# A second routed FFN merged into the program of a recurrence, its gelus cut into halves behind two scan steps

## The chip, the cores and the metric

The kernel runs on one core of a Trainium2 chip. The metric is the device time of one execution in microseconds (us). The profile is of one more execution; its time is given beside its span.

## What is computed

The input x has 4 sequences of 1024 positions and 128 features, in float32. `ln` is a layer norm without weights.

```python
x = x + 0.5 * L0_ffn(ln(x))     # routed FFN: per position a small attention over the 4 sequences,
                                # then top 2 of 8 experts, gelu (tanh form), 128 -> 256 -> 128
x = x + L0_attn(ln(x))          # hierarchical attention
x = x + 0.5 * L0_ffn(ln(x))     # the same routed FFN again
x = x + 0.5 * L1_ffn(ln(x))     # binarised weights, exact gelu, 128 -> 512 -> 128     ("a")
x = x + L1_attn(ln(x))          # recurrence over the 1024 positions                   ("p", "r")
x = x + 0.5 * L1_ffn(ln(x))     # the binarised FFN again                              ("z")

def step(state, inp):           # inside L1_attn, 1024 times, state [4 x 32]
    xb_t, xd_t = inp
    state = tanh(state @ A.T + xb_t)
    return state, state @ C.T + xd_t
# then y = layernorm(out + x) * w + b, and y + gelu(y W1 + b1) W2 + b2
```

Each routed FFN acts on a position by itself. So do the FFNs a and z. Only the recurrence has an order over positions.

## The kernel before

x stays in SBUF as `x_all`, in 8 groups of 128 positions by 4 sequences. The kernel is written for each engine by hand, with semaphores, and runs four programs one after the other (`PHASES`, L1947): routed FFN (`causal_moe_ffn`, L31), attention, routed FFN, and then `binarize` (L546) with `second_half` (L597). A program begins when all engines have ended the one before.

**The routed FFN** works through the 8 groups. For each of 8 experts PE makes two chunks of hidden values (`up_products`, L270, one product of 512 columns a chunk, in a ring of three PSUM banks), ScalarE makes each chunk's gelu in one instruction of 512 columns (L193), PE multiplies back (`down_products`, L279, 8 products of 128 columns into one of two banks), and VectorE adds the expert with its weight into x (`add_expert`, L456). Between the experts stand the steps of later groups: transposes (`p_turn1`, `p_turn2`, `p_turn3`), the query-key-value product (`p_qkv`, L239, two banks in turn), projection and router, and their norms on VectorE with the power -1/2 on GpSimd.

**`second_half`** holds the scan. `body(g)` (L921 on PE, L997 on ScalarE) is made for each group g and has 128 steps. A step is one product on PE, `r_scan<-r_state,rnnA` (L941: 4 columns, 32 outputs), and one tanh on ScalarE (L1006) whose result is the next step's input. After each step's product stands at most one other piece of PE work, at the step that the table `SLOTS` gives it: a product or transpose of 128 columns. The pieces of body g are a(g+2), p(g+1), r(g-1) and z(g-1): `turn_piece`, `up_piece`, `down_piece`, `mix_piece`, `input_piece`. ScalarE makes each gelu of those FFNs as four instructions of 128 columns behind four tanhs (`gelu_piece`). Each engine executes its instructions in the order written, so that a wait of one holds up all behind it, the scan's too.

The last group's r and z come after the last step.

Of the kernel before, what the change touches and what calls it, by code (L numbers as in the profile page):

```python
# [545 lines left out]
def binarize(nc, S):  # L546

    with ExitStack() as ctx:
        sgn = ctx.enter_context(nc.sbuf_tensor("sgn", [128, 2, FC, 128], F32))
        alpha = ctx.enter_context(nc.sbuf_tensor("alpha", [128, FC + 1], F32))  # L550
        banks = [ctx.enter_context(nc.psum_tensor(f"bin_turn{i}", [128, 512], F32)) for i in range(2)]
        s_sign, s_bin, s_turn = (ctx.enter_context(nc.semaphore(n)) for n in ("signs", "binarised", "bin_turned"))
        w1 = S["bin1"][:, :].rearrange("p (c d) -> p c d", d=D)
        w2 = S["bin2"][:, :].rearrange("p (c h) -> p c h", h=128)
        with nc.Block() as block:
            @block.scalar
            def _(act):
                for i, w in enumerate((w1, w2)):
                    nc.scalar.activation(sgn[:, i, :, :], w, ACT.Sign).then_inc(s_sign, 1)

            @block.vector
            def _(dve):

                dve.tensor_reduce(alpha[:, 0:FC], w1, AX.X, ALU.add, apply_absolute_value=True)
                dve.tensor_reduce(alpha[:, FC:FC + 1], w2, AX.XY, ALU.add, apply_absolute_value=True)
                dve.drain()
                dve.tensor_scalar(alpha[:, 0:FC], alpha[:, 0:FC], 1.0 / D, None, ALU.mult)
                dve.tensor_scalar(alpha[:, FC:FC + 1], alpha[:, FC:FC + 1], 1.0 / (FC * 128), None, ALU.mult)
                dve.drain()
                dve.wait_ge(s_sign, 2)  # L570
                for i, w in enumerate((w1, w2)):
                    for c in range(FC):
                        a = alpha[:, c:c + 1] if i == 0 else alpha[:, FC:FC + 1]
                        dve.scalar_tensor_tensor(sgn[:, i, c, :], sgn[:, i, c, :], a, w[:, c, :],
                                                 ALU.mult, ALU.subtract)
                dve.drain()
                for i, w in enumerate((w1, w2)):
                    dve.tensor_tensor(sgn[:, i, :, :], sgn[:, i, :, :], w, ALU.add).then_inc(s_bin, 1)

                rows = S["rows"]  # L580
                dve.tensor_tensor(rows[:, 1, :], rows[:, 1, :], rows[:, 2, :], ALU.add)
                dve.tensor_scalar(rows[:, 3, :], rows[:, 3, :], 0.5, None, ALU.mult)
                for i, n in enumerate(("bin1", "bin2")):
                    dve.wait_ge(s_turn, i + 1)
                    dve.tensor_copy(S[n][:, :], banks[i][:, :])

            @block.tensor
            def _(pe):
                for i in range(2):
                    pe.wait_ge(s_bin, i + 1)  # L590
                    for c in range(FC):
                        last = nc.tensor.transpose(banks[i][:, c * 128:(c + 1) * 128], sgn[:, i, c, :],
                                                   S["ident"][:, :])
                    last.then_inc(s_turn, 1)
# [1384 lines left out]
```

## Time and profile before

| | us |
|---|---|
| median of 3 runs | 2226.37 (2222.71 to 2226.94) |
| the profiled execution | 2226.66 |
| its span, first to last instruction | 2224.9 |
| PE busy | 1851.9 (83%) |
| DVE busy | 1009.9 (45%) |
| ACT busy | 862.7 (39%) |
| POOL busy | 193.9 (9%) |
| mean granted TensorE clock | 0.735 |

All times inside the program are us from the span's start. A granted clock of 1.00 is 2.4 GHz and one of 0.50 is 1.2 GHz, the two levels that occur; a mean between them says that a stretch had both. PE is TensorE's products, PEld its weight loads, DVE is VectorE, ACT ScalarE, POOL GpSimd. A float32 product leaves two MATMUL records and two LDWEIGHTS records, a float32 transpose one of each. "Busy" counts a record from its issue to its end.

### The profile page before, as it was taken

The numbers are of one execution on the slowest core, as the hardware profiler recorded it, in microseconds if no ns is written. First come the engines' busy times: TensorE is split into PE (matmuls) and PEld (weight loads), VectorE is DVE, ScalarE is ACT, GpSimd is POOL, SyncE is SP. The second block draws the span as 40 slices with busy tenths as digits, with TensorE's granted clock in tenths as the row PEclk, the third lists the DMA queues.
The fourth block names the chain that finished last, engine by engine and source line by source line (L and its number), as shares of the span: only waits on it lengthen the run. The fifth ranks groups of instructions, "written<-read, shape, count | busy, mean of one in ns | idle before, by whom it ended". The sixth has DMA issues, their size and how long they took to land. (4 is left out here: it accounts for less than half of the span.)

```text
span 2224.9 us, 37410 instructions
## 1 busy us (share of the span) xinstructions
PE 1851.9 (83%) x13672; PEld 1372.4 (62%) x13672; DVE 1009.9 (45%) x3005; ACT 862.7 (39%) x2377; POOL 193.9 (9%) x314
## 2 busy tenths in 40 slices
PE   1889896848858588558898977799999999999886
PEld 1666675447556485546666765576777777766665
DVE  3666754775866778746666642111111111111102
ACT  1434442745546456424353432232323232323231
POOL 1211201001010010012121100000000000000000
PEclk8999996969879799779999985555555555555556
DMA  6000000000000000000000000000000000000000
GB/s 156 1 1 0 0 1 1 2 1 3 2 1 3 2 2 2 1 1 1 1 0 1 1 1 1 1 1 5 1 6 1 5 1 5 1 5 1 5 1 10
DMA packets 12015, 13.03 MB, mean 6 GB/s; under 512 B 1648, under 2 KB 10640, under 8 KB 11280
## 3 DMA queue, kind: packets, MB, share of 16 engines
q1 hardware_dynamic: 11840, 10.77, 1.8%
q8 instruction: 101, 1.65, 0.3%
q14 instruction: 74, 0.61, 0.1%
HBM read 8.67 MB, written 2.10 MB: 5 GB/s over the span
## 5 line engine op out<-in xcount | busy, mean ns | idle before, releaser
L1006 ACT ACTIVATE r_state<-r_scan 32x4 f32<-32x4 f32 x1024 | 166.9, 163 | 592.6 <-PE r_scan L941 589.3
L941 PEld LDWEIGHTS r_scan<-r_state,rnnA 128*32 128x32 f32 x2048 | 186.3, 141 | 253.3 <-issue 153.6
L941 PE MATMUL r_scan<-r_state,rnnA 128*32 128x4 f32 x2048 | 275.4, 205 | 52.1 <-ACT r_state L1006 52.1
L286 PEld LDWEIGHTS f_down<-moe,f_hT 128*128 128x128 f32 x2048 | 251.3, 194 | 56.9 <-issue 54.0
L277 PE MATMUL f_up<-f_x2T,moe 128*128 128x512 f32 x512 | 248.8, 610 | 11.6 <-ACT f_hT L193 11.6
L286 PE MATMUL f_down<-moe,f_hT 128*128 128x128 f32 x2048 | 254.0, 278 | 0.0
L463 DVE SCALAR_TENSOR_TENSOR x_all<-f_down,f_weight,x_all 128x128 f32 (+1 forms) x512 | 144.1, 344 | 166.6 <-PE f_down L286 163.9
L193 ACT ACTIVATE f_hT<-f_up 128x512 f32<-128x512 f32 x256 | 149.9, 598 | 139.0 <-PE f_up L277 137.6
L1618 DVE TENSOR_TENSOR att_big<-at_ring,att_big 128x512 f16<-128x512 f32 x192 | 123.9, 685 | 49.2 <-ACT att_big L1300 48.4
L277 PEld LDWEIGHTS f_up<-f_x2T,moe 128*128 128x128 f32 x512 | 90.5, 195 | 90.0 <-issue 63.5
L1300 ACT ACTIVATE att_big<-at_ring 128x512 f16<-128x512 f32 x192 | 111.4, 596 | 66.5 <-PE at_ring L1433 64.6
L761 DVE TENSOR_TENSOR x_all<-r_post_misc,x_all 128x512 f32<-128x512 f32 x8 | 5.5, 692 | 233.4 <-PE r_post_misc L845 233.4
L1433 PE MATMUL at_ring<-at_keys,att_Mhi 128*128 128x512 f16 x256 | 81.7, 403 | 30.2 <-DVE at_coarse_q L1605 18.6
L833 PE MATMUL r_up_post<-r_nT_r,mlp 128*128 128x128 f32 x256 | 94.9, 483 | 1.3 <-DVE r_nT_r L725 0.9
L845 PE MATMUL r_post_misc<-bin,r_h_post 128*128 128x128 f32 x256 | 93.1, 474 | 1.2 <-ACT r_h_post L976 1.2
L845 PE MATMUL r_post_misc<-mlp,r_h_post 128*128 128x128 f32 x256 | 93.1, 474 | 1.2 <-ACT r_h_post L976 1.2
L1725 DVE SCALAR_TENSOR_TENSOR att_big<-at_ring,att_big 128x512 f16<-128x512 f32 x128 | 80.8, 682 | 27.2 <-ACT att_big L1341 27.1
L1523 PE MATMUL at_s<-att_Nhi,att_big 128*128 128x128 f16 x1024 | 92.8, 222 | 0.0
L1341 ACT ACTIVATE att_big<-at_ring 128x512 f16<-128x512 f32 x128 | 68.7, 602 | 61.4 <-PE at_ring L1514 61.0
L1523 PE MATMUL at_s<-att_Nlo,att_big 128*128 128x128 f16 x512 | 89.3, 222 | 0.0
L1452 PEld LDWEIGHTS at_s<-at_keys,att_big 128*128 128x128 f16 x768 | 64.5, 99 | 38.4 <-issue 19.5
L1452 PE MATMUL at_s<-at_keys,att_big 128*128 128x16 f16 x768 | 72.1, 172 | 18.5 <-DVE att_big L1618 18.5
(241 smaller groups left out, 3202.2 us busy)
## 6 DMA issues: line engine op xcount, KB each, us to landing
x_all<-in_x SPq DMA_DIRECT2D x4, 512.0 KB, 6.1
moe<-in_moe SPq DMA_DIRECT2D x2, 1024.0 KB, 7.1
out<-x_all SPq DMA_DIRECT2D x8, 256.0 KB, 2.3
bin<-in_bin SPq DMA_DIRECT2D x2, 256.0 KB, 7.6
mlp<-in_mlp SPq DMA_DIRECT2D x2, 256.0 KB, 6.0
att_big<-in_att_wq SPq DMA_DIRECT2D x1, 512.0 KB, 11.2
att_big<-in_att_wk SPq DMA_DIRECT2D x1, 512.0 KB, 13.2
att_big<-in_att_wv SPq DMA_DIRECT2D x1, 512.0 KB, 14.9
```

The source lines that it names most:

```text
L193: nc.scalar.activation(hT[c % H_RING][:, :], up[c % UP_RING][:, :], ACT.Gelu_apprx_tanh).then_inc(s_h, 1)
L277: nc.tensor.matmul(up[c % UP_RING][:, :], w1[:, c * 128:(c + 1) * 128], x2T[b][:, :], start=True, stop=True).then_inc(s_up, 1)
L286: last = nc.tensor.matmul(down[e % 2][:, s * 128:(s + 1) * 128], hT[c % H_RING][:, s * 128:(s + 1) * 128], w2[:, c * 128:(c + 1) * 128], s ...
L463: last = dve.scalar_tensor_tensor(xg[:, s, :], down[e % 2][:, s * 128:(s + 1) * 128], weight[b][:, s, e:e + 1], xg[:, s, :], ALU.mult, ALU ...
L833: ins = nc.tensor.matmul(UP[k][c % len(UP[k])][:, s * 128:(s + 1) * 128], W1[k][:, c * 128:(c + 1) * 128], nT[k][g % 2][:, s * 128:(s + 1) ...
L845: ins = nc.tensor.matmul(MISC[k][:, s * 128:(s + 1) * 128], H[k][c][:, s * 128:(s + 1) * 128], W2[k][:, c * 128:(c + 1) * 128], start=(c = ...
L941: nc.tensor.matmul(scan[b][0:STATE, NB * t:NB * (t + 1)], rnnA[:, :], last, start=False, stop=(t == 127), skip_group_check=True).then_inc( ...
L1006: nc.scalar.activation(state[b][0:STATE, NB * t:NB * (t + 1)], scan[b][0:STATE, NB * t:NB * (t + 1)], ACT.Tanh).then_inc(s_tanh, 1)
L1300: nc.scalar.activation(XH[c % 2][:, :, h, :], ring[n % RING][:, :].rearrange("p (q i) -> p q i", i=BLK), ACT.Copy).then_inc(s_xhi, 1)
L1452: nc.tensor.matmul(o, lh, keys[:, blk, 0, :], start=True, stop=False)
L1523: last = nc.tensor.matmul(sbk[t % 2][:, 0:D], y[t % 2][:, h, :], att[w][:, h * D:(h + 1) * D], start=(h == 0 and n == 0), stop=(h == HEADS ...
L1618: dve.tensor_tensor(XL[c % 2][:, :, h, :], ring[n % RING][:, :].rearrange("p (q i) -> p q i", i=BLK), XH[c % 2][:, :, h, :], ALU.subtract) ...
```

## The change

The third and fourth program become one, `routed_ffn_and_recurrence`. It computes the same. The second routed FFN runs two groups ahead of the scan: groups 0 and 1 before the first step, group m = g + 2 inside body g, for g from 0 to 5. The binarised weights are prepared at the program's start. Body g also holds a(g+1), p(g+1), r(g-1) and z(g-2); before, it was a(g+2), p(g+1), r(g-1), z(g-1). z of group 6, r of 7 and z of 7 come after the last step.

With one program there are 8 PSUM banks for all: two for the scan, two for `up` (a ring of three before), one `down` (two before), one `turn` for every transpose and small product of the routed FFN (three before), and `post_misc` and `pre_misc`. The FFNs a, r and z use `up`, `up` and `down` in turn.

The order on PE is no longer a table of steps. `slots(g)` writes the items of a body in a row with a length in ns for each and spreads them evenly over the 128 steps. An item is larger than a piece: half a chunk (256 columns), an expert's tile (2 products of 128 columns), a dense tile (4 such products), all four transposes of a group. Gelus are two instructions of 256 columns behind two tanhs.

```diff
-PHASES = ("ffn", "attn", "ffn", "second")
+PHASES = ("ffn", "attn", "rest")
...
+            def p_turn1(pe, f):
+                pe.wait_ge(s_xn1, ONE + f + 1)
+                pe.wait_ge(s_stats2, ONE + f)
+                turn_tiles(xn1, s_turn1, turn)
...
+            def p_qkv(pe, f, s):
+                if s == 0:
+                    pe.wait_ge(s_ln1T, ONE + f + 1)
+                pe.wait_ge(s_qkv, ONE + NB * f + s)
+                nc.tensor.matmul(turn[:, 0:QKV], ln1T[:, s * 128:(s + 1) * 128], wqkv[:, :],
+                                 start=True, stop=True).then_inc(s_q, 1)
...
+            def down_tile(pe, m, e, s):
+                if s == 0:
+                    pe.wait_ge(s_h, ONE + CHUNKS * m + 2 * e + 2)
+                    pe.wait_ge(s_add, ONE + EXPERTS * m + e)
...
+            def k_up_half(pe, k, g, c, half, before):
...
+                    elif before is None:
+                        m = clip(g + 2 if k == "a" else GROUPS)
+                        pe.wait_ge(s_h, ONE + CHUNKS * m)
+                        pe.wait_ge(s_add, ONE + EXPERTS * m)
...
+            NS = {up_half: 480, down_tile: 500, k_turn_tiles: 1000, p_turn1: 1000, p_turn2: 1000, p_turn3: 1000,
+                  p_qkv: 740, p_proj: 1000, p_router: 500, k_up_half: 480, k_down_tile: 1000, input_product: 900,
+                  mix_tiles: 1000}
...
+            def slots(g):
+                order = routed_order(g + 2, g) + dense_order(g)
+                total, at, out_ = sum(NS[f] for f, _ in order), 0, []
+                for f, args in order:
+                    out_.append((int(128 * (at + NS[f] / 2) / total), f, args))
+                    at += NS[f]
+                return out_
...
+                    for t in range(128):
+                        last = state[b][:, NB * (t - 1):NB * t] if t else state[1 - b][:, 512 - NB:512]
+                        pe.wait_ge(s_tanh, ONE + 128 * g + t)
+                        nc.tensor.matmul(scan[b][0:STATE, NB * t:NB * (t + 1)], rnnA[:, :], last, start=False,
+                                         stop=(t == 127), skip_group_check=True).then_inc(s_step, 1)
+                        run([(f, args) for at, f, args in plan if at == t])
...
+                        part = slice(256 * half, 256 * half + 256)
+                        ins = nc.scalar.activation(hT[c % H_RING][:, part], up[c % 2][:, part], ACT.Gelu_apprx_tanh)
...
+                    for at, f, args in plan:
+                        if f is up_half and args[2]:
+                            m, c = args[:2]
+                            p += [(until(until(at + 1 + half, down_tile, m, c // 2), up_half, m, c + 2), gelu, (m, c, (half,)))
+                                  for half in range(2)]
```

On VectorE `v_after(m+1)`, which reads the projection out of `turn` and gives the signal `s_stats2`, stands behind `add_expert(m, 3)`, as before.

The order on PE in the scan, before: one piece behind each step's product. `r_up_post` is a bank of hidden values, `r_tanh_done` the signal of the tanh.

```order
L833 MATMUL r_up_post<-r_nT_r,mlp 128x128
L941 MATMUL r_scan<-r_state,rnnA 32x4 [waits r_tanh_done]
L833 MATMUL r_up_post<-r_nT_r,mlp 128x128 [waits r_h_r,r_nT_r]
L941 MATMUL r_scan<-r_state,rnnA 32x4 [waits r_tanh_done]
L833 MATMUL r_up_post<-r_nT_r,mlp 128x128
L941 MATMUL r_scan<-r_state,rnnA 32x4 [waits r_tanh_done]
```

And now, in body 3, from the last tiles of expert 3 (`m_down`) over the projection of group 6 (`m_turn<-wproj`), the transposes of group 7 (`m_turn<-ident,m_xn`) and those of r of group 2, to the next expert's first half chunk (`m_up`). "x2" at a scan product says that a step holds nothing else.

```order
L1337 MATMUL m_scan<-m_state,rnnA 32x4 [waits m_tanh_done]
L1168 MATMUL m_down<-moe,m_hT 128x128 x2
L1337 MATMUL m_scan<-m_state,rnnA 32x4 [waits m_tanh_done]
L1130 MATMUL m_turn<-wproj,m_headsT 128x128 [waits m_headsT_done]
L1130 MATMUL m_turn<-wproj,m_headsT 128x128 x3
L1337 MATMUL m_scan<-m_state,rnnA 32x4 [waits m_tanh_done] x2
L1103 MATMUL m_turn<-ident,m_xn 128x128 [waits m_stats2_done,m_xn1_done]
L1103 MATMUL m_turn<-ident,m_xn 128x128 x3
L1337 MATMUL m_scan<-m_state,rnnA 32x4 [waits m_tanh_done] x2
L1103 MATMUL m_post_misc<-ident,m_xn_r 128x128 [waits m_xn_r]
L1103 MATMUL m_post_misc<-ident,m_xn_r 128x128 x3
L1337 MATMUL m_scan<-m_state,rnnA 32x4 [waits m_tanh_done]
L1158 MATMUL m_up<-m_x2T,moe 128x256 [waits m_h_done]
```

The steps now hold twice to four times as much, and a transpose in the row waits for VectorE's `stats2`. The order on ScalarE in the same body, where the routed part ends and the dense part begins:

```order
L1484 ACTIVATE m_state<-m_scan 32x4 [waits m_step_product] x7
L1407 ACT_TABLE_LOAD
L1407 ACTIVATE m_probs<-m_shifted 128x256 [waits m_scores_shifted]
L1422 ACTIVATE m_gate<-m_shifted_g 128x32 [waits m_logits_shifted]
L1484 ACTIVATE m_state<-m_scan 32x4 [waits m_step_product] x2
L1440 ACT_TABLE_LOAD [waits m_down_a]
L1440 ACTIVATE m_h_a<-m_up,chunk_bias 128x256 [waits m_up_a]
L1484 ACTIVATE m_state<-m_scan 32x4 [waits m_step_product]
L1440 ACTIVATE m_h_a<-m_up,chunk_bias 128x256
```

Table loads, an exponential and half gelus now stand between tanhs; before, only gelus of 128 columns did.

## Rows read from the trace of the kernel before

**Rows 1.** The table of stretches: second routed FFN, binarize, bodies 0 to 7, end.

```profile
core 0: us, PE busy (x) PEld busy (x) DVE busy (x) ACT busy (x) POOL busy (x), PEclk, DMA share, GB/s
968.00:1015.60 47.60, 19.68 (x54) 11.29 (x54) 21.62 (x85) 9.12 (x17) 14.38 (x24) 0.64 0.00 0
1015.60:1089.10 73.50, 70.08 (x392) 50.93 (x392) 51.01 (x209) 33.22 (x54) 15.30 (x26) 0.98 0.00 1
1089.10:1304.00 214.90, 200.09 (x1123) 144.34 (x1122) 132.68 (x550) 89.48 (x146) 31.80 (x54) 0.97 0.00 1
1304.00:1346.20 42.20, 26.14 (x158) 23.65 (x158) 20.69 (x74) 11.27 (x35) 4.83 (x8) 0.72 0.01 1
...
1651.70:1762.30 110.60, 109.59 (x489) 79.27 (x488) 18.86 (x62) 33.10 (x177) 5.09 (x8) 0.50 0.01 3
...
2177.30:2224.90 47.60, 28.40 (x152) 24.85 (x152) 11.77 (x34) 9.18 (x33) 2.41 (x4) 0.71 0.04 12
```

**Rows 2.** The tanhs, all 1024 of them.

```profile
L1006 ACT ACTIVATE r_state<-r_scan x1024: 162/163/165, 1346.2 to 2177.3; 32x4 f32<-32x4 f32 x171
```

**Rows 3.** The timeline of two steps with a product of 128 columns (start, us).

```profile
1643.04 0.50 PEld L845 LDWEIGHTS r_post_misc<-bin,r_h_post 128*128 128x128 f32 x2
...
1643.14 0.16 ACT L1006 ACTIVATE r_state<-r_scan 32x4 f32<-32x4 f32 x1 [0.76 <-PE r_scan L941]
1643.76 0.18 PEld L941 LDWEIGHTS r_scan<-r_state,rnnA 128*32 128x32 f32 x2 [0.22 <-issue]
1643.76 0.27 PE L941 MATMUL r_scan<-r_state,rnnA 128*32 128x4 f32 x2
1643.96 0.50 PEld L845 LDWEIGHTS r_post_misc<-bin,r_h_post 128*128 128x128 f32 x2
1643.96 0.80 PE L845 MATMUL r_post_misc<-bin,r_h_post 128*128 128x128 f32 x2
1644.07 0.16 ACT L1006 ACTIVATE r_state<-r_scan 32x4 f32<-32x4 f32 x1 [0.76 <-PE r_scan L941]
```

**Rows 4.** The timeline of steps that hold nothing, at 1.2 GHz, PE alone.

```profile
2095.08 0.27 PE L941 MATMUL r_scan<-r_state,rnnA 128*32 128x4 f32 x2 [0.25 <-ACT r_state L1006]
2095.60 0.27 PE L941 MATMUL r_scan<-r_state,rnnA 128*32 128x4 f32 x2 [0.25 <-ACT r_state L1006]
```

**Rows 5.** The timeline of steps at 2.4 GHz, the first with a transpose.

```profile
1348.84 0.23 PE L941 MATMUL r_scan<-r_state,rnnA 128*32 128x4 f32 x2
...
1348.99 0.33 PE L860 MATMUL r_pre_misc<-ident,r_xn_a 128*128 128x128 f32 x1
...
1349.31 0.22 PE L941 MATMUL r_scan<-r_state,rnnA 128*32 128x4 f32 x2
```

**Rows 6.** Products back to back, at 1.2 GHz and at 2.4 GHz.

```profile
1340.05 2.29 PE L845 MATMUL r_pre_misc<-bin,r_h_pre 128*128 128x128 f32 x9
...
2198.42 3.84 PE L845 MATMUL r_post_misc<-mlp,r_h_post 128*128 128x128 f32 x32 [1.23 <-ACT r_h_post L976]
```

**Rows 7.** The table of stretches around the changes of the clock.

```profile
1317.20:1324.00 6.80, 6.02 (x27) 5.62 (x28) 2.97 (x13) 2.28 (x8) 1.21 (x2) 0.50 0.00 1
1324.00:1334.30 10.30, 8.90 (x76) 8.46 (x76) 3.33 (x11) 4.80 (x19) 0.31 (x2) 1.00 0.00 1
...
1344.50:1351.30 6.80, 4.31 (x35) 3.05 (x34) 4.24 (x15) 1.30 (x8) 1.21 (x2) 1.00 0.00 0
1351.30:2191.00 839.70, 782.11 (x3604) 563.60 (x3604) 125.86 (x402) 247.44 (x1336) 32.65 (x52) 0.50 0.01 3
```

**Rows 8.** VectorE's timeline in the routed FFN: add, `v_after` with its statistics.

```profile
1224.59 1.13 DVE L463 SCALAR_TENSOR_TENSOR x_all<-f_down,f_weight,x_all 128x128 f32 x4 [1.17 <-PE f_down L286]
1225.63 0.68 DVE L401 TENSOR_TENSOR f_after<-f_turn,f_hs 128x512 f32<-128x512 f32 x1
1226.39 0.87 DVE L405 BATCH_NORM_STATS2 f_stats<-f_after 128x6 f32<-128x128 f32 x4
1227.33 0.38 DVE L408 BATCH_NORM_AGGREGATE f_mv<-f_stats 128x2 f32<-128x6 f32 x4
```

**Rows 9.** ScalarE's groups in the routed FFN, groups 2 to 7.

```profile
L193 ACT ACTIVATE f_hT<-f_up 128x512 f32<-128x512 f32 x96 | 56.2, 598 | 55.2 <-PE f_up L277 54.8
...
L168 ACT ACTIVATE f_qkv<-f_qkvb 128x384 f32<-128x384 f32 x16 | 7.9, 491 | 10.0 <-PE f_qkvb L245 10.0
L193 ACT ACT_TABLE_LOAD x6 | 7.7, 1283 | 3.6 <-PE f_up L277 2.7 <-PE f_down L286 1.0
```

**Rows 10.** The mix products after the last step, at 1.2 GHz: starts of successive ones.

```profile
2178.89 0.83 PE L878 MATMUL r_post_misc<-rnnD,r_nT_p 128*128 128x128 f32 x2
...
2179.66 0.83 PE L878 MATMUL r_post_misc<-rnnC,r_state 32*128 32x128 f32 x2
```

More of the change, by code:

```diff
@@ L543, in layouts_second_half @@
     }
[L546 to L594, printed above, removed]
@@ new lines, in v_after @@
+                def v_after(g):
+                    dve.wait_ge(s_proj, ONE + g + 1)
+                    dve.tensor_tensor(after[:, :, :], turn[:, :].rearrange("p (s d) -> p s d", d=D),
+                                      hs[g % 2][:, :, :], ALU.add)
+                    dve.drain()
+                    for s in range(NB):
+                        dve.bn_stats(stats2[:, s, :], after[:, s, :])
+                    dve.drain()
+                    for s in range(NB):
+                        last = dve.bn_aggr(mv2[:, s, :], stats2[:, s, :])
+                    last.then_inc(s_stats2, 1)
@@ new lines, in add_expert @@
+                def add_expert(g, e):
+                    dve.wait_ge(s_down, ONE + EXPERTS * g + e + 1)
+                    dve.wait_ge(s_add, ONE + EXPERTS * g + e)
+                    for s in range(NB):
+                        last = dve.scalar_tensor_tensor(grp(g)[:, s, :], down[:, s * 128:(s + 1) * 128],
+                                                        weight[g % 2][:, s, e:e + 1], grp(g)[:, s, :],
+                                                        ALU.mult, ALU.add)
+                    last.then_inc(s_add, 1)
@@ new lines, in routed @@
+                    if own:
+                        add_expert(m, 1)
+                    if back:
+                        v_heads(m + 1)
+                    if own:
+                        add_expert(m, 2)
+                    if front:
+                        v_norm1(m + 2)
+                    if post:
+                        k_norm("r", g - 1, mixed)
+                    if own:
+                        add_expert(m, 3)
+                    if back:
+                        v_after(m + 1)
@@ new lines, in routed @@
+                    if own:
+                        add_expert(m, 5)
+                    if (m, g) == (1, -1):
+                        k_norm("p", 0, grp(0))
+                    if front:
+                        v_scores(m + 2)
+                    if own:
+                        add_expert(m, 6)
+                    if front:
+                        v_shift(m + 2)
+                    if back:
+                        v_logits(m + 1)
+                    if (m, g) == (1, -1):
+                        v_nT("p", 0)
@@ new lines, in _ @@
+                for g in range(GROUPS):
+                    routed(g + 2, g)
+                    dense(g)
+                g = GROUPS
+                v_nT("z", g - 2)
+                v_mix(g - 1)
+                k_norm("r", g - 1, mixed)
+                v_update_bin("z", g - 2)
+                v_nT("r", g - 1)
+                v_resid(g - 1)
+                v_update_mlp(g - 1)
+                k_statistics("z", g - 1, grp(g - 1))
+                k_norm("z", g - 1, grp(g - 1))
+                v_nT("z", g - 1)
@@ L1926, in macaron_kernel @@
                 att_ctx.close()
-            if ph == "second":
-                binarize(nc, S)
-                second_half(nc, S, out, s_store, "r")
+            if ph == "rest":
+                routed_ffn_and_recurrence(nc, S, out, s_store)
                 return
```

895 lines of the change are left out of this document (647 added, 248 removed).

## Prediction

> **What bounds the kernel now.** I read the table of stretches first. The second routed FFN takes 968.0 to 1304.0 with PE busy nearly throughout and, past its first 47.6 us, a clock of 0.97 to 0.98; binarize and the scan's front take 42.2 us; a body of the scan takes 110.6 us with PE busy 109.6 of it at 0.50, which is 1.2 GHz [rows 1]. The 1024 tanhs run from 1346.2 to 2177.3, 831.1 us in all [rows 2].
>
> The timeline of a step shows what "busy" hides. A step with one product of 128 columns takes 0.92 us (weight load to weight load), and ScalarE waits 0.76 us of it for PE [rows 3]: PE sets the end. A step that holds nothing takes 0.52 us at 1.2 GHz [rows 4] and 0.47 us at 2.4 GHz [rows 5], the round trip of product and tanh. Back to back, nine records take 2.29 us at 1.2 GHz [rows 6] where two take 0.80 [rows 3]: 1.49 us for seven, 0.213 a record, 0.427 a product of 128 columns. So 0.50 us of each loaded step of 0.92 is the price of putting the scan's product between others. At 2.4 GHz, 32 records take 3.84 us [rows 6], at most 0.24 a product; I take 0.22.
>
> The clock is the second fact. It rose after PE had run products back to back (1317.2 to 1324.0, then 1.00), held 1.00 over the first steps and fell to 0.50 as the steps ran empty, and then stayed at 0.50 for 839.7 us, though nearly every step had its product [rows 7].
>
> **The change, part by part.** All sums are against the profiled execution, 2226.7 us, 0.3 us above the median of the runs.
>
> *Front.* It gives back the stretch from 1089.1 (group 2's first gelu) to 1346.2: 257.1 us. It adds: signs and scales on VectorE ahead of the first norm, and single banks that make PE wait for ScalarE's copies of 0.49 us [rows 9] between query-key-value products, some 10 us in the 47.6 us before the first gelu; two groups with such waits, 4 to 5 us each; a and p of group 0 between the tiles, some 12 us. Together 31 us, bounds 15 and 50 (the whole 42.2 us of rows 1 is above what the same a and p work costs). Net 226 us less.
>
> *Rest.* z of group 6 moves behind the last step: some 6 us more on top of 47.6 [rows 1].
>
> *Bodies.* With 831.1 us taken out as well, 1176 us stand outside the bodies: 2226.7 - 226 - 831.1 + 6. I count products of 128 columns in body 3: routed up 64 and down 64, dense up 48 and down 48, transposes 14, query-key-value 12, mix 8, projection 4, input 4, together 266, where it now has 116. They stand in 108 steps; 20 hold nothing.
>
> - At 1.2 GHz: 266 x 0.427 = 113.6, 108 x 0.50 = 54, 20 x 0.52 = 10.4.
> - At 2.4 GHz: 266 x 0.22 = 58.5; of the 0.50 us, the 0.20 from the scan's product to the next load [rows 3] becomes 0.15 [rows 5], and no row shows the other 0.30 (half of it or all may stay), so 0.36 x 108 = 39; 20 x 0.475 = 9.5.
>
> To this come waits. The new one is `p_turn1` on `s_stats2`: after expert 3's last tile VectorE adds for 1.13 us, then runs `v_after` for 2.1 us (1225.63 to 1227.71) [rows 8], with signals 3.4 us; PE has the projection and an empty step meanwhile, 1.7 us at 2.4 GHz. So PE, with the scan behind it, waits 1.7 us. Two of the four query-key-value products wait 0.8 us for a tanh and a copy; the first dense half chunk waits 1.0 us for expert 7's add; mix products cost 0.76 us, not 0.43 [rows 10], 2.6 us for eight at 1.2 GHz; the router's 8 short products 0.9 us. Three table loads of 1.28 us [rows 9] stand between tanhs; at 1.2 GHz an item of 0.85 to 1.7 us covers most of each, at 2.4 GHz about 3 us show. Sum 9 us at 1.2 GHz, 12 us at 2.4 GHz. Body 3 is then 187 or 119 us. Two half gelus of some 0.4 us (0.598 for a whole one [rows 9]) hide behind PE's items; were they whole, ScalarE with tanh and gelu would need 0.76 us of a step of 0.8 us at 2.4 GHz.
>
> The page "ScalarE: Activation LUTs" of the Trainium skill, under Terms, gives a table load some 2.7 us. By that figure a body at 2.4 GHz would be 4 us longer, an estimate; the trace has 1.28 us, and the sum goes by it.
>
> By the same count (products / loaded steps): body 0 190/88, 1 232/103, 2 as 3, 4 252/107, 5 244/107 give at 1.2 GHz 151, 173, 187, 187, 178, 174, sum 1050; at 2.4 GHz 100, 112, 119, 119, 112, 109, sum 671. Bodies 6 (116/43) and 7 (76/28) have no routed part; nearly empty, I hold them at 1.2 GHz: 117 + 101 = 218. The method gives 113.6 us for today's body 3, measured 110.6, so it is some 3% high. All bodies at 1.2 GHz: 1176 + 1050 + 218 = 2444. Bodies 0 to 5 at 2.4 GHz: 2065. The clock alone decides the sign.
>
> **Where I chose.** The scan is entered at 2.4 GHz, after dense work. The wait at `p_turn1` leaves PE some 2.5 us with nothing but two scan products, as empty as the steps with which the clock fell [rows 5, 7]; I count on a fall there in bodies 0 to 3. Whether it comes back between scan products no row shows: with 0.43 of 0.92 us in products it never did, back to back it did [rows 3, 7]. The changed bodies have 0.85 of 1.35 us in most steps and 1.7 of 2.2 us in the double and dense ones, between the two. I take the middle: it comes back somewhere late in a body, most likely among the dense tiles, and holds until the next `p_turn1`. That is 0.6 of the steps of bodies 0 to 3 at 2.4 GHz, and 0.9 in bodies 4 and 5, which have no `p_turn1`. It saves 0.6 x (51 + 61 + 68 + 68) = 149 and 0.9 x (66 + 65) = 118 from 2444: 2177 us, taken as **2178**.
>
> **Rivals.**
> 1. *The clock does not come back between scan products.* For it: 839.7 us at 0.50 with PE "busy" 782 [rows 7]. Against: each step now streams twice as much or more. The first third of body 0 stays fast: 2444 - 17 = 2427 us, 9% slower. It decides as soon as fewer than some 0.57 of the steps of bodies 0 to 5 run at 2.4 GHz ((2444 - 2227) / 379).
> 2. *The clock stays up.* The wait is too short or covered, or the clock is back within a few steps: 2065 us. For it: the first steps did run at 1.00 [rows 7]. The page "TensorE: Matmul & The Clock Gate" of the Trainium skill, in its part on the clock gate, says that activity releases the throttle, and this gives that time if the denser steps are activity enough; no run here shows it for such steps.
> 3. *Another bound.* ScalarE has per body 128 tanhs of 0.163, 56 half gelus of some 0.4 and some 9 us of others, 52 us; VectorE 132.7 / 6 + 18.9 = 41 us [rows 1]. Neither reaches 119 us, so this only lengthens waits.
> 4. *It doesn't do what it says.* The order shows the merged bodies, so no.
>
> The 0.50 us gap is the other doubt. The clock page says, in Step-by-step, that PE pulls weight loads ahead of products in flight. If that hid the first load behind the scan's product, a step would lose some 0.16 us, 17 us a body (an estimate). Rows 3 show the load after the scan's product in today's steps, and the sum keeps it.
>
> **How the numbers follow.** Forecast 0.40, with its own range 2110 to 2270; rival 1 0.37, 2385 to 2465; rival 2 0.19, 2030 to 2100; 0.04 for the rest. A measurement tells about 0.2% from no change, 4.5 us. Of the forecast's 0.40, 0.29 lies below 2222, 0.02 within and 0.09 above. Faster: 0.29 + 0.19 + 0.03 = 0.51; same 0.03; slower: 0.09 + 0.37 = 0.46. Leaving out the ends of both rivals, some 0.18, gives 2050 to 2440.
>
> **What would show it.** Right: bodies 0 to 3 some 145 us each with granted clocks between 0.70 and 0.85, a fall at the transposes behind `m_turn<-wproj`, bodies 4 and 5 near 117. Rival 1: six bodies of 151 to 187 us at 0.50. Rival 2: none over 120 us. The model itself is wrong if a step with one half chunk at 1.2 GHz isn't 1.35 us, if the first step doesn't come near 1120 us, or if PE waits long anywhere I have not named.

## The result and the profile after

| | us |
|---|---|
| changed kernel, median of 4 runs | 2379.27 (2356.86 to 2396.58) |
| kernel before, beside it, 4 runs | 2225.97 (2222.71 to 2226.94) |
| ratio, 95% interval | 1.066 (1.058 to 1.073) |
| the profiled execution, its span | 2378.39, 2376.6 |
| mean granted TensorE clock | 0.705 (before 0.735) |

The change makes the kernel 6.6% slower; 2178 was forecast. Ratios here and below leave out executions in a slower state, so they can lie a little under the ratio of the medians (1.069 here). The time lies inside the range (2050 to 2440), on the side of the first rival.

The table of stretches of the changed kernel, bodies 0 to 7 and the end (columns as in [rows 1]):

```profile
1126.70:1281.90 155.20, 135.32 (x549) 90.02 (x549) 39.55 (x172) 40.26 (x181) 12.44 (x21) 0.51 0.00 1
1281.90:1453.70 171.80, 160.32 (x617) 107.08 (x618) 42.24 (x159) 43.28 (x189) 11.23 (x19) 0.50 0.00 1
1453.70:1612.70 159.00, 149.39 (x668) 100.49 (x668) 42.55 (x161) 45.89 (x196) 12.44 (x21) 0.63 0.00 1
1612.70:1766.50 153.80, 142.41 (x668) 96.01 (x668) 44.86 (x167) 45.81 (x197) 12.44 (x21) 0.68 0.01 3
1766.50:1935.00 168.50, 159.95 (x656) 110.44 (x656) 38.55 (x145) 43.55 (x190) 6.04 (x10) 0.56 0.01 2
1935.00:2104.10 169.10, 160.51 (x632) 107.39 (x632) 27.92 (x94) 41.05 (x186) 4.83 (x8) 0.52 0.01 2
2104.10:2223.20 119.10, 94.51 (x440) 64.71 (x440) 16.96 (x51) 29.46 (x153) 3.62 (x6) 0.51 0.01 3
2223.20:2325.10 101.90, 74.91 (x374) 51.03 (x374) 11.01 (x34) 26.41 (x144) 2.41 (x4) 0.50 0.01 3
2325.10:2376.60 51.50, 35.61 (x172) 29.14 (x172) 13.28 (x37) 10.23 (x25) 2.42 (x4) 0.80 0.06 16
```

Bodies 0 to 5 take 977.4 us together at clocks of 0.50 to 0.68. With c the mean clock, the share of time at 2.4 GHz is 2c - 1: 0.02, 0, 0.26, 0.36, 0.12 and 0.04. Steps are shorter at 2.4 GHz, so the share of steps is larger: counted in the trace, 4, 0, 48, 63, 18 and 9 of each body's 128 tanhs start at 2.4 GHz, 142 of 768. The tanhs answer to [rows 2]: the first comes 219.5 us earlier, at 1126.7 (1120 was forecast), the last 147.8 us later.

```profile
L1484 ACT ACTIVATE m_state<-m_scan x1024: 146/163/165, 1126.7 to 2325.1; 32x4 f32<-32x4 f32 x171
```

The model of a step holds. In the timeline of PE, body 3, a step with one item takes 1.36 us at 1.2 GHz (1641.95 to 1643.31) and 0.80 at 2.4 GHz (1660.30 to 1661.10). `p_turn1`'s transposes wait 1.99 us there and 1.56, 1.55 and 1.64 us in bodies 0 to 2 (forecast 1.7). The z transposes at the body's start wait 1.44 us, which I had not named. The profile shows no releaser; by the code they wait for VectorE's last add of the z before (`k_x["z"]`), and that add ended at 1613.97, 0.11 us ahead of them:

```profile
1614.08 0.63 PE L1103 MATMUL m_post_misc<-ident,m_xn_z 128*128 128x128 f32 x4 [1.44 <-issue]
...
1641.95 0.27 PE L1337 MATMUL m_scan<-m_state,rnnA 128*32 128x4 f32 x2
1642.15 1.22 PE L1158 MATMUL m_up<-m_x2T,moe 128*128 128x256 f32 x2
1643.31 0.27 PE L1337 MATMUL m_scan<-m_state,rnnA 128*32 128x4 f32 x2
...
1660.30 0.23 PE L1337 MATMUL m_scan<-m_state,rnnA 128*32 128x4 f32 x2
1660.45 0.71 PE L1168 MATMUL m_down<-moe,m_hT 128*128 128x128 f32 x4
1661.10 0.23 PE L1337 MATMUL m_scan<-m_state,rnnA 128*32 128x4 f32 x2
...
1667.42 0.63 PE L1103 MATMUL m_turn<-ident,m_xn 128*128 128x128 f32 x4 [1.99 <-DVE m_mv L828]
```

Longer unnamed waits, 3.0 and 4.3 us, stand ahead of transposes of r and p in bodies 6 and 7; these two bodies took 221 us, forecast 218.

What failed is the clock. The stretches around its changes:

```profile
1112.00:1130.20 18.20, 15.42 (x105) 12.90 (x105) 13.17 (x56) 8.48 (x21) 4.51 (x6) 1.00 0.01 1
...
1130.20:1505.70 375.50, 344.24 (x1334) 229.53 (x1334) 93.15 (x364) 93.65 (x417) 27.96 (x49) 0.50 0.00 1
...
1577.40:1614.90 37.50, 32.98 (x230) 24.09 (x230) 9.91 (x34) 13.52 (x62) 2.42 (x4) 1.00 0.00 0
...
1652.50:1669.50 17.00, 14.25 (x102) 10.70 (x102) 8.32 (x32) 6.13 (x29) 1.21 (x2) 1.00 0.01 2
1669.50:1731.00 61.50, 58.15 (x210) 36.95 (x210) 17.24 (x65) 17.21 (x69) 4.53 (x6) 0.50 0.00 1
1731.00:1775.30 44.30, 38.99 (x258) 28.17 (x258) 10.07 (x31) 16.59 (x71) 2.41 (x4) 1.00 0.02 7
```

It fell at 1130.2, with the fifth scan product of body 0, and stayed down for 375.5 us with PE "busy" 344 of them. The timeline just ahead of the fall shows a table load and a half gelu of ScalarE between two tanhs, and PE's scan product waiting for them:

```profile
1128.23 0.16 ACT L1484 ACTIVATE m_state<-m_scan 32x4 f32<-32x4 f32 x1 [0.62 <-PE m_scan L1337]
1128.41 1.28 ACT L1431 ACT_TABLE_LOAD   x1
...
1129.70 0.38 ACT L1431 ACTIVATE m_hT<-m_up 128x256 f32<-128x256 f32 x1
1129.98 0.15 ACT L1484 ACTIVATE m_state<-m_scan 32x4 f32<-32x4 f32 x1
...
1130.18 0.27 PE L1337 MATMUL m_scan<-m_state,rnnA 128*32 128x4 f32 x2 [0.85 <-ACT m_state L1484]
```

Into body 3 the clock came high and fell at 1614.9, behind the 1.44 us that PE waited for z's transposes. It came back at 1652.5, just behind a step with two half chunks, fell at 1669.5 behind `p_turn1`'s wait, as forecast, and came back at 1731.0 among the dense tiles. It then lasted to 1775.3, the first steps of body 4.

The whole scan has seven falls. Two come at `p_turn1`'s wait (1512.5 and 1669.5), one behind the table load (1130.2), one behind z's transposes (1614.9), one behind the 1.25 us that the first dense half chunk of body 4 waits (1867.5), one in a row of mix products (1775.3) and one in nearly empty steps (2106.4). A wait doesn't settle it: z's transposes wait 1.44 us in body 4 too (1767.82), and there the clock stayed up for 7.5 us more. The six returns (1505.7, 1577.4, 1652.5, 1731.0, 1857.3, 2096.2) all come at most one loaded step behind a step of 1.7 to 2.2 us that holds two items or the input products; but 115 steps at 1.2 GHz were longer than 1.9 us, and most brought nothing. So all parts of the forecast picture occur, but the clock also falls at places I had priced in time alone or not named, and the return is rare.

### The profile page after: what moved, and what is told of

It is laid out like the page before. It is cut to its first block, busy times and chain, and to the rows that moved or that the text cites. A ratio compares the mean times of both kernels' runs of the same rounds, so it can differ in the third digit from the quotient of the medians.

```text
span 2376.6 us, 36746 instructions
## 1 busy us (share of the span) xinstructions
PE 1950.8 (82%) x13544; PEld 1399.0 (59%) x13544; DVE 1011.2 (43%) x3005; ACT 838.2 (35%) x2320; POOL 193.8 (8%) x314
## 4 chain that ended last, share of the span: by engine, by line
issue 54%; POOL 3%; POOLq 2%; PE 0%; DVE 0%; ACT 0%; ACTq 0%; SPq 0%; DVEq 0%
POOL m_pairs L706 1%; POOLq L673 1%; POOL m_roots L697 0%; POOL m_root_r L716 0%; POOLq L715 0%; POOL m_root_a L716 0%; POOL m_root_p L716 0%; POOL m_root_z L716 0%; PE m_post_misc L1220 0%; PE m_up L1209 0%; POOLq L688 0%; POOL m_roots L690 0%; POOLq L684 0%; POOLq L686 0%; PE m_down L1209 0%
## 5 line engine op out<-in xcount | busy, mean ns | idle before, releaser
L1484 ACT ACTIVATE m_state<-m_scan 32x4 f32<-32x4 f32 x1024 | 166.8, 163 | 884.1 <-PE m_scan L1337 882.8
L1337 PEld LDWEIGHTS m_scan<-m_state,rnnA 128*32 128x32 f32 x2048 | 181.0, 136 | 408.9 <-issue 269.5
L1337 PE MATMUL m_scan<-m_state,rnnA 128*32 128x4 f32 x2048 | 269.5, 202 | 85.6 <-ACT m_state L1484 85.6
L1158 PE MATMUL m_up<-m_x2T,moe 128*128 128x256 f32 x512 | 259.7, 625 | 1.5 <-ACT m_hT L1431 1.5
L1168 PE MATMUL m_down<-moe,m_hT 128*128 128x128 f32 x1024 | 254.2, 402 | 3.8 <-DVE x_all L882 3.8
L1168 PEld LDWEIGHTS m_down<-moe,m_hT 128*128 128x128 f32 x1024 | 200.9, 281 | 8.2 <-issue 4.2
L286 PEld LDWEIGHTS f_down<-moe,f_hT 128*128 128x128 f32 x1024 | 125.4, 194 | 28.3 <-issue 27.0
L277 PE MATMUL f_up<-f_x2T,moe 128*128 128x512 f32 x256 | 123.8, 608 | 5.8 <-ACT f_hT L193 5.8
L1158 PEld LDWEIGHTS m_up<-m_x2T,moe 128*128 128x128 f32 x512 | 121.5, 283 | 11.5 <-ACT m_hT L1431 2.6
L286 PE MATMUL f_down<-moe,f_hT 128*128 128x128 f32 x1024 | 126.7, 278 | 0.0
```

The lines of the kernel that those rows point to most:

```text
L277: nc.tensor.matmul(up[c % UP_RING][:, :], w1[:, c * 128:(c + 1) * 128], x2T[b][:, :], start=True, stop=True).then_inc(s_up, 1)
L286: last = nc.tensor.matmul(down[e % 2][:, s * 128:(s + 1) * 128], hT[c % H_RING][:, s * 128:(s + 1) * 128], w2[:, c * 128:(c + 1) * 128], s ...
L1158: ins = nc.tensor.matmul(up[c % 2][:, part], w1[:, c * 128:(c + 1) * 128], x2T[m % 2][:, part], start=True, stop=True)
L1168: ins = nc.tensor.matmul(down[:, s * 128:(s + 1) * 128], hT[c % H_RING][:, s * 128:(s + 1) * 128], w2[:, c * 128:(c + 1) * 128], start=(c ...
L1337: nc.tensor.matmul(scan[b][0:STATE, NB * t:NB * (t + 1)], rnnA[:, :], last, start=False, stop=(t == 127), skip_group_check=True).then_inc( ...
L1484: nc.scalar.activation(state[b][0:STATE, NB * t:NB * (t + 1)], scan[b][0:STATE, NB * t:NB * (t + 1)], ACT.Tanh).then_inc(s_tanh, 1)
```

## The experiments

Three theories. **A**: the clock is the whole loss; a scan product after each item or two leaves PE at 1.2 GHz, and more PE work between scan products brings 2.4 GHz back. **B**: the new waits and single banks cost the time. **C**: each loaded step costs its 0.50 us whatever the clock. All kernels run beside the kernel before; its median was 2227 to 2230 us each time. All edits are to the changed kernel unless said.

### e1 and e2: the same items in rows

```diff
-out_.append((int(128 * (at + NS[f] / 2) / total), f, args))
+out_.append((int(128 * (at + NS[f] / 2) / total) // 4 * 4, f, args))
```

> The items of a body are moved to every fourth step: some four items stand back to back behind one scan product, and the three steps after it are empty. Work, instructions and waits are the same. Priced at 1.2 GHz, body 3 has 266 products x 0.427 + 32 loaded steps x 0.50 + 96 empty x 0.52 = 179.5 us against 178 as changed: nothing gained. Theory A (what the change lost is the clock: a scan product after every item or two keeps PE at 1.2 GHz, back to back it rises): bodies 0 to 5 run mostly at 2.4 GHz, body 3 some 125 us (58.5 + 32 x 0.36 + 96 x 0.475 = 115.6, and 9 us of waits), bodies 0 to 5 together 680 to 780 us where the changed kernel has 977, and the whole kernel 2080 to 2190. Theory B (the new waits and single banks are what costs): they are all still there and meet more work at once, so the time stays at 2378 or rises by up to 30 us. Theory C (each loaded step costs 0.50 us, whatever the clock): an empty step costs as much, 2378 +- 10.

Measured: 2306.1 us (2287.8 to 2308.6), ratio to before 1.034 (1.030 to 1.038). That is 73 us less than the changed kernel, with the same work; C, by which rows change nothing, and B, by which they only cost, are out as the whole explanation. Body 3, and the worst step of the profile, where projection and `p_turn1` stand in one row:

```profile
1594.20:1761.40 167.20, 128.17 (x669) 98.82 (x669) 45.82 (x166) 43.91 (x196) 12.45 (x21) 0.71 0.01 2
```

```profile
1646.70 1.09 PE L1103 MATMUL m_turn<-ident,m_xn 128*128 128x128 f32 x4 [2.62 <-DVE m_mv L828]
...
1648.02 0.16 ACT L1484 ACTIVATE m_state<-m_scan 32x4 f32<-32x4 f32 x1 [4.84 <-PE m_scan L1337]
```

The mean clock went from 0.705 to 0.784. But the total missed A's 2080 to 2190: waits grew, as B said (2.62 us for 1.99 at this place, the tanh 4.84 us late), and the transposes behind the wait already run at 1.2 GHz (1.09 us for the four, 0.63 above). Here a wait cost its own time and the clock behind it.

e2 makes the rows two steps long (`// 2 * 2`).

> As e1, but every second step: two items back to back, then one empty step. At 1.2 GHz two steps are 2.22 + 0.52 = 2.74 us against 2 x 1.35 = 2.70. Theory A: a double step of 2.2 us is no more than what the dense part of the changed kernel already had, where the clock rarely came back, so little changes: 2330 to 2390, and clearly more than e1. Theory B: as changed, 2378 to 2390. Theory C: 2378 +- 10. If bundling helps for another reason than a long row of products (fewer switches between scan and items), half of e1's gain would come.

Measured: 2402.4 us (2348.9 to 2424.4). The four executions lie 75 us apart, so rows of two neither gain nor lose anything that can be told. The profiled one is the slowest: its body 3 took 189.5 us at a clock of 0.50, yet its body 4 had 0.70. The median is 12 us above the expectation, which stays open.

### e3: the transposes wait for the read alone

```diff
 dve.tensor_tensor(after[:, :, :], turn[:, :]..., hs[g % 2][:, :, :], ALU.add)
+    .then_inc(s_read, 1)
...
-pe.wait_ge(s_stats2, ONE + f)
+pe.wait_ge(s_read, ONE + f)
```

> The transposes behind the projection wait for VectorE's read of the projection and no longer for its statistics: the step of p_turn1 shrinks from 2.84 us by some 0.9 us (0.87 + 0.38 us of statistics, less what overlaps), six places. Theory A: the clock mostly is at 1.2 GHz ahead of these places anyway, so 6 x 0.9 = 5 us come back, 2368 to 2378, and the share of 2.4 GHz in the bodies stays under 0.3. Theory B, and the prediction's place for the fall (the clock falls at p_turn1 and would stay up without it): bodies 2 and 3, where it fell there, go on at 2.4 GHz to their end, 20 to 60 us less.

Measured: four executions of 2275.3, 2327.2, 2328.6 and 2389.2 us, median 2327.9. Their mean clocks are 0.747, 0.724, 0.723 and 0.695: the same program differs by 114 us, and the time follows the clock. The profiled one is the slowest, with body 3 at 0.55.

Three of the four lie below every run of the changed kernel, by more than the 5 us that A allowed. Some 7 us of it lie ahead of the scan, whose first tanh starts at 1120.1 and not at 1126.7, since the groups before it have the same wait. So the wait at `p_turn1` seems to cost the clock in part of the executions; how much on average can't be told from a spread of this size.

### e4: whole gelus

```diff
-for half in halves: ... nc.scalar.activation(hT[...][:, part], up[c % 2][:, part], ...)   # 256 columns
+nc.scalar.activation(hT[c % H_RING][:, :], up[c % 2][:, :], ACT.Gelu_apprx_tanh)       # 512 columns
```

The gelus of a, r and z are made whole in the same way.

> Each gelu is one instruction of 512 columns behind one tanh, not two of 256 behind two. ScalarE then has 0.163 + 0.6 us behind one tanh; at 1.2 GHz a step with one half chunk is 1.35 us, so it hides: 2378 +- 8 (a few fixed costs less, ScalarE's busy time some 20 us less). At 2.4 GHz the step of 0.79 us would be stretched by some 0.1 us, which the few stretches at 2.4 GHz hardly show. If instead the halves are what costs (more instructions between tanhs), 2350 or less; if they protect the scan even at 1.2 GHz, over 2400.

Measured: 2372.4 us (2366.3 to 2398.2) against the changed kernel's 2379.3: the same within their spreads. At 1.2 GHz the halving neither costs nor protects anything that these runs can tell. At 2.4 GHz, for which the halves were meant, no run tests them.

### e5: rows without the waits

The items of a body are written as rows by hand, as the expectation tells; gelus and copies are placed anew, and e3's shorter wait is in it too.

```diff
+rows_ += [A(0, 1, 2), A(3) + R(0, 1), kd(a, "a", g + 1, 0, 1), ...]
+if e == 4:
+    B = only(real(f), p_turn1, f) + B + only(a, k_turn_tiles, "a", g + 1)
+if e == 5 and real(f):
+    A = q[0] + up(12) + q[1] + up(13)
+    B = q[2] + dn(e, (0, 1)) + q[3] + dn(e, (2, 3))
...
+out_.append((128 * at // sum(cost), row))
```

> The changed kernel with a new order inside the bodies alone: PE's items in rows of about four (four half chunks; four tiles of an expert; two dense tiles), each row behind one scan product and spaced by its own length; p_turn1 an expert later than its projection and waiting for the read of turn only; query-key-value products apart; mix tiles in rows; gelus, copies and exponentials behind the tanh of a step that holds a row, where ScalarE is free, not behind those of empty steps. e1 showed at 2.4 GHz 3.4 us lost at the step with projection and p_turn1, 0.9 at the query-key-value products, 1.3 at step 1 and 4.9 at steps 80 and 81 (table loads), and 0.1 to 0.7 where gelus stood behind tanhs of empty steps; its clock fell at each of these places. Theory A: with these waits gone the clock stays at 2.4 GHz over most of bodies 0 to 5 (share 0.75 or more, e1 0.5), body 3 120 to 135 us, the kernel 2090 to 2230. Theory B (waits alone, no clock): their sum is some 12 us a body, so 2306 - 60 = 2245 to 2290 with the clock share as in e1.

Measured: 2229.1 us (2222.8 to 2237.3), ratio 1.001 (0.9998 to 1.0025). Body 3:

```profile
1548.80:1688.70 139.90, 112.81 (x669) 89.26 (x670) 44.19 (x166) 48.08 (x196) 12.40 (x21) 0.83 0.01 3
```

It lies at the edge of A's range, and below B's (2245 to 2290). But most of the step from e1 is waiting saved, as B has it. Bodies 0 to 5 of e1, then of e5:

```profile
1127.10:2033.30 906.20, 683.70 (x3789) 521.29 (x3790) 238.15 (x896) 249.80 (x1137) 59.45 (x100) 0.75 0.01 2
```

```profile
1120.10:1956.10 836.00, 667.69 (x3789) 527.41 (x3790) 234.77 (x896) 270.18 (x1136) 59.26 (x100) 0.78 0.01 2
```

They shrank by 70 us. The waits that the profile lists for PE in them sum to 222 us in e1 and 168 in e5, 54 us less, while the clock rose from 0.75 to 0.78 only, a share of time at 2.4 GHz of 0.56 where A asked for 0.75. So the new order, waits and placement together, gives back the whole loss of 150 us; e5 by itself doesn't say how much of its gain over e1 is clock.

### e6 and e9: useless products in the empty steps

```diff
 run([(f, args) for at, f, args in plan if at == t])
+if 0 < t < free and not any(at == t for at, _, _ in plan):
+    nc.tensor.matmul(scan[1 - b][0:EXPERTS, 0:128], wrouter[:, :], wqkv[:, 0:128], start=True, stop=True)
```

`free` is the step of the input product. e6 is e1 with this, e9 the same with 16 columns (`0:16`).

> e1 with useless work: in each step without an item, up to the input product, PE makes one product of 128 columns that nobody reads (8 columns of weights, 128 rows), into the scan's idle bank. Nothing else is changed. PE does 0.22 us (2.4 GHz) or 0.43 us (1.2 GHz) more in each such step, of which an empty step leaves 0.25 us free while ScalarE makes the tanh. Theory A (PE's own activity sets its clock): the share of 2.4 GHz rises from e1's 0.5 to over 0.8 in bodies 0 to 5 and, in bodies 6 and 7, from near 0 to most of it; the kernel gets FASTER for more work: 2100 to 2230, depending on what a filler's weight load costs the next scan product (0 to 0.15 us in some 95 steps a body). Theory B and C: useless products can only cost: 96 x 0.1 to 0.25 us a body, 8 bodies, 2380 to 2500.

> Control for e6 (2168 us, against e1's 2306): the same filler products at the same places with the same weight loads and the same number of instructions, but 16 columns each and not 128. Theory A (it is the streaming of columns that keeps PE's clock up): almost nothing of e6's gain is left, 2280 to 2310, and an empty step still takes 0.48 or 0.52 us. If the mere presence of an instruction in the empty steps does it (PE not idle, weights being loaded), the time is e6's, 2160 to 2180.

Measured: e6 2168.2 us (2160.7 to 2175.6), ratio 0.973 (0.970 to 0.976); e9 2294.7 us (2284.5 to 2300.9), ratio 1.028 (1.024 to 1.031). Bodies 3 and 6 of e6, then of e9:

```profile
1534.90:1676.50 141.60, 123.41 (x843) 81.85 (x843) 45.79 (x166) 43.86 (x197) 12.42 (x21) 0.93 0.01 3
...
1938.20:2031.50 93.30, 85.35 (x605) 50.26 (x606) 16.40 (x49) 28.39 (x152) 3.61 (x6) 0.86 0.01 4
```

```profile
1588.50:1751.50 163.00, 129.60 (x843) 98.19 (x843) 45.84 (x166) 43.97 (x196) 12.41 (x21) 0.75 0.01 2
2024.70:2142.90 118.20, 96.51 (x605) 68.58 (x605) 16.40 (x49) 29.37 (x153) 3.62 (x6) 0.52 0.01 3
```

This decides it. Both have the same instructions (x843 and x605 on PE in these bodies); only the columns of the useless products differ, and 126 us hang on them. More work made the kernel 138 us faster than e1, which B and C exclude. The timeline of e6 shows what a filler costs, first a step at 2.4 GHz, then one at 1.2 GHz:

```profile
1562.36 0.23 PE L1338 MATMUL m_scan<-m_state,rnnA 128*32 128x4 f32 x2
1562.44 0.38 PE L1342 MATMUL m_scan<-wqkv,wrouter 128*8 128x128 f32 x2
1562.83 0.23 PE L1338 MATMUL m_scan<-m_state,rnnA 128*32 128x4 f32 x2
```

```profile
1550.44 0.27 PE L1338 MATMUL m_scan<-m_state,rnnA 128*32 128x4 f32 x2
1550.57 0.59 PE L1342 MATMUL m_scan<-wqkv,wrouter 128*8 128x128 f32 x2
1550.97 0.21 PE L1338 MATMUL m_scan<-m_state,rnnA 128*32 128x4 f32 x1
```

A step with a filler takes 0.47 us at 2.4 GHz and 0.53 at 1.2 GHz, where empty ones took 0.48 (changed kernel, 1664.73 to 1665.21) and 0.52 [rows 4]: it runs while ScalarE makes the tanh, and is free.

### e10: fillers alone

The changed kernel in its own order, with e6's filler in its empty steps.

> The changed kernel in its own order, items spread singly, with e6's filler of 128 columns in the steps that hold nothing: 20 steps in body 3, 85 in body 6, 100 in body 7. In e6 a filler step took 0.478 us at 2.4 GHz and 0.520 at 1.2 GHz, as an empty one: free. Theory A: bodies 6 and 7 go to 2.4 GHz for most of their length as in e6 (93 and 84 us against 119 and 102), 40 us less; in bodies 0 to 5 most steps hold an item and get no filler, so they stay mostly at 1.2 GHz and gain 0 to 60 us: 2280 to 2345. If fillers alone were enough and the rows of four not needed, 2170 or less.

Measured: 2227.7 us (2198.0 to 2243.0), ratio 0.994 (0.990 to 0.998). Bodies 0, 3 and 6:

```profile
1134.60:1249.80 115.20, 104.44 (x627) 65.18 (x627) 39.83 (x172) 40.06 (x181) 12.50 (x21) 0.84 0.00 1
```

```profile
1545.90:1699.00 153.10, 145.65 (x700) 96.69 (x700) 44.85 (x167) 45.90 (x197) 12.42 (x21) 0.69 0.01 2
1991.30:2083.20 91.90, 84.13 (x580) 49.53 (x580) 16.92 (x50) 28.64 (x152) 3.62 (x6) 0.87 0.01 4
```

Body 6 gained 27 us as expected. The total missed the range on the good side by 52 us, as bodies 0 to 5 gained 121 us (977 to 857) where 60 were allowed; body 0 alone gained 40 (115.2 for 155.2), its clock at 0.84 for 0.51 with fillers in 39 of its steps. So fillers alone, like the new order alone (e5), give back the whole loss. Body 3, with 16 fillers in 128 steps (x700 for x668; the empty steps behind the input product get none), stayed at 0.69, where e6, with rows and 87 fillers, has 0.93.

### e7 and e11: both together

e7 is e5 with e6's fillers.

> e5 with e6's filler products. Theory A: bodies 0 to 7 at 2.4 GHz almost throughout, body 3 120 to 140 us, bodies 6 and 7 some 75 to 95 us where they have 119 and 102: 2010 to 2150, faster than the kernel before the change (2227). Theory B and C: slower than e5 by 80 to 200 us.

> e7 (2078 us) with the two mix tiles of a body no longer at its start in one row of 1.5 and one of 3 us, but each ahead of a row of an expert's work. In e7 the clock fell at each body's start (mix tiles, table load) and came back some eight to ten steps later, once or twice a body. Theory A: a mix row and its neighbours keep it up or it comes back within a few steps; six bodies x 1 to 4 us: 2055 to 2078. Same as e7 if the table load alone does it.

e7 took 2078.3 us (2074.8 to 2085.0), ratio 0.932 (0.931 to 0.934). In e11 the mix tiles move:

```diff
-rows_ += [zt + up(0) + up(1) + only(r, mix_tiles, g - 1, 0), only(r, mix_tiles, g - 1, 1)]
+rows_ += [zt + up(0) + up(1)]
...
+if e == 0:
+    A, B = only(r, mix_tiles, g - 1, 0) + A, only(r, mix_tiles, g - 1, 1) + B
```

It took 2078.2 us (2069.1 to 2079.1), ratio 0.931 (0.928 to 0.933): no different from e7, so the mix tiles were not worth it. Its bodies 3, 4 and 7:

```profile
1482.60:1609.20 126.60, 121.28 (x853) 82.01 (x854) 44.18 (x166) 48.09 (x196) 12.41 (x21) 0.95 0.01 3
1609.20:1730.00 120.80, 115.28 (x839) 77.58 (x840) 38.46 (x144) 45.05 (x190) 6.03 (x10) 0.99 0.01 3
...
1944.70:2026.80 82.10, 79.37 (x604) 40.88 (x603) 11.08 (x33) 26.60 (x144) 2.41 (x4) 0.92 0.02 4
```

These are the fastest kernels of the study, 7% faster than before and 13% faster than the changed kernel.

### e8, e12 and e13: the kernel before, without the merge

```diff
-"input": [30, 31, 32, 33],
+"input": [124, 125, 126, 127],
...
-return p
+return [(at // 8 * 8 if at < 128 else at, f, args) for at, f, args in p]
...
+if t and not any(at == t for at, _, _ in plan):
+    dst = scan[1 - b] if t < free else up_post[0]
+    nc.tensor.matmul(dst[0:8, 0:128], W1["a"][:, 0:8], W1["a"][:, 0:128], start=True, stop=True)
```

The gelu pieces are moved to every eighth step in the same way. e13 leaves out the last three lines.

> The kernel BEFORE the change (nothing merged) with its pieces moved to every eighth step (eight products in a row; the input product last in the body), its quarter gelus likewise, and one filler product of 128 columns in each step that holds nothing. Its bodies ran at 1.2 GHz throughout, 110.6 us for body 3. Theory A: the clock comes back and holds: body 3 is 116 x 0.22 + 16 x 0.36 + 112 x 0.475 = 84.5 us if fillers are free, 100 with 0.14 us each: 2227 - 8 x (10 to 26) = 2020 to 2150. Then the merge itself was not needed for the gain. If the fillers cost 0.3 us or more in a step, or the clock stays at 1.2 GHz, it is 2230 to 2500.

> e8 again (the kernel before the change, pieces in rows of eight, fillers in the empty steps; 2115 us), with the filler's bank chosen by where the input product stands, since in e8 body 1's fillers fell into the scan's next inputs. The instructions are the same in number and length: 2105 to 2125. It is the fair partner of e7 and e11: with the clock held up in both, the merge is worth the difference, which the sums put at 37 us (2115 - 2078).

> The kernel before the change with its pieces in rows of eight and no fillers: e12 without its useless products. At 1.2 GHz this costs nothing: 0.92 + 0.52 us for a loaded and an empty step against one of 0.5 + 2 x 0.427 and one of 0.52, the same. Theory A: in a row of eight products the clock may rise for a part of the row and falls again in the seven empty steps: a share of 2.4 GHz under 0.3 and 0 to 60 us gained, 2165 to 2235. If rows alone are what made e12 fast, 2130 or less.

e8 took 2115.0 us; in its body 1 fillers overwrite part of the scan's inputs, so it computes something else. e12, where they don't, took 2112.7 us (2108.2 to 2118.5), ratio 0.948 (0.945 to 0.950). e13, rows without fillers, took 2273.3 us (2269.4 to 2276.6), ratio 1.020 (1.016 to 1.024). Body 3 of e12, then of e13:

```profile
1611.40:1704.60 93.20, 88.51 (x714) 52.02 (x713) 18.71 (x61) 33.53 (x177) 5.08 (x8) 0.98 0.01 4
```

```profile
1667.50:1786.70 119.20, 88.46 (x489) 71.93 (x489) 18.71 (x61) 33.97 (x177) 5.08 (x8) 0.56 0.01 3
```

Here the rows alone lost 43 us, though the clock rose to 0.56. The waits for the tanh don't explain it: PE waited 29.5 us for it in 112 steps of body 3, but 112 empty steps at the 0.25 us of an empty step [rows 4] are 28 us of that. The expectation priced every loaded step of before at 0.92 us. The trace of before has cheaper ones, here a transpose at 1.2 GHz:

```profile
1671.30 0.27 PE L941 MATMUL r_scan<-r_state,rnnA 128*32 128x4 f32 x2
1671.50 0.48 PE L860 MATMUL r_pre_misc<-ident,r_xn_p 128*128 128x128 f32 x1
1671.90 0.27 PE L941 MATMUL r_scan<-r_state,rnnA 128*32 128x4 f32 x2
```

Such a step takes 0.61 us, and one with an input product 0.53, where an empty one takes 0.52. These 20 of body 3's pieces, the 16 transposes and 4 input products, were nearly free between scan products, and in a row they cost their own length. That is part of the 8.6 us that body 3 lost; the rest stays open. The fillers are worth 160 us. They take body 3 from 110.6 [rows 1] to 93.2 us in a kernel that merges nothing.

## Why the prediction was wrong

*The first step's place and the work outside the bodies* were right: 1126.7 for 1120, and 2378.4 - 1198.4 = 1180 us outside the bodies for 1176.

*The price of a step* was right at both levels: 1.36 for 1.35 us, 0.80 for the 0.80 that 0.44 + 0.36 gives; so the 0.36 us taken for the gap at 2.4 GHz, between the bounds, was met. That was in part luck, as no row before gave it. An empty step at 2.4 GHz was read from [rows 5], whose first step holds a transpose; empty ones of the changed kernel take 0.48 us, so the sum stands.

*The sum at 1.2 GHz* was good: body 1, at 0.50 throughout, took 171.8 for 173 us.

*Where I chose* is the step that failed: "0.6 of the steps of bodies 0 to 3 at 2.4 GHz, and 0.9 in bodies 4 and 5". Measured are 0.03, 0, 0.38, 0.49 and 0.14, 0.07 of the steps, 0.18 over the six bodies. Put into the same sum they save 2 + 0 + 26 + 33 + 9 + 5 = 75 us for the 267 forecast, and 2444 - 75 = 2369, 10 us below the measured 2379. So this one number is some 190 of the 201 us of the miss.

It failed in two ways. The fall was tied to `p_turn1` alone, which has two of the seven falls. The clock also fell behind a table load between tanhs (0.85 us of waiting at PE, in the fifth step, where rival 1 had the first third of body 0 fast), behind z's transposes in body 3, and twice in body 4, among its mix products and behind its first dense half chunk. I had listed table loads as 3 us of time and asked nothing of the clock behind them; and body 4, which I thought safe for lack of `p_turn1`, has such places too. That each of these waits by itself brings the clock down is read from what stands next to the falls, not tested. And the return was taken from the middle between two known rows, 0.43 of 0.92 us and back to back. The runs order this gap: among single items it came back six times in the scan, rows of two were no better (e2, within its spread), rows of four bring it back for part of a body (e1), fillers in the few empty steps do so too (e10), and rows with the empty steps filled hold it at 0.93 to 0.99 in bodies 0 to 5 (e11). e9 shows that the columns of the fillers make the difference: with 16 columns they gain 11 us on e1, with 128 they gain 138.

*Rival 1* is what nearly happened: 2427, with its own range from 2385; the run came out 6 us below that.

*Rival 2*, all bodies at 2.4 GHz, was priced at 2065. e11, in another order and with fillers, comes close to it and takes 2078: bodies 0 to 5 took 724 us for 671, at clocks of 0.93 to 0.99; bodies 6 and 7 178 for 218, since fillers hold the clock there too. With the clock up the merged kernel is faster than before, with the clock down slower, as the sum said.

*What the merge is worth*, with the clock held up on both sides: 2112.7 - 2078.2 = 34.5 us. This is for these two orders: e11's was written by hand around the waits, e12's only moves the old pieces to every eighth step. The larger part of e11's gain was to be had without merging. *The halves of the gelus* are worth nothing measurable at 1.2 GHz (e4).

## What to carry to other kernels

When a long serial chain runs beside other PE work, price a wait for its own time and ask what the clock does behind it; look up in the trace what stood ahead of each fall and each return, and don't interpolate between a row that never brought it back and one that always did. If PE idles while another engine makes the chain's next value, fill that idle time with products nobody reads; here a filler of 128 columns with 8 columns of weights fitted in for nothing. Long rows of the other work helped the merged kernel and cost the old one 2% by themselves, so try them together with fillers. Do that first, before a large rewrite: on the old kernel it gave 5% with a dozen lines.
